# Experts of a small mixture: the second product with the expert's matrix standing still, rows packed and turned in pairs

## The chip, the cores and the metric

The kernel runs on one core of one Trainium2 chip. The metric is the device time of the whole program in microseconds (us), the median of several runs. The core has five engines that work side by side and are held together by semaphores: TensorE (PE in the profile, with PEld for the loading of the stationary operand), VectorE (DVE), ScalarE (ACT), GpSimd (POOL) and SyncE (SP, whose queue carries most DMAs).

## The reference, cut to what matters

The program is one block of a network: a token-pruning attention and, after it, a layer with 8 experts. The change is in the expert layer:

```python
# x: T = 16 * 3136 tokens of D = 64; E = 8 experts, F = 256, C = ceil(1.25 * T / E) = 7840 seats each
idx = argmax(softmax(x @ gate_w + gate_b)); prb = the largest probability
pos = the token's number among those of its expert; kept = pos < C
buf[idx, pos] = x                                         # where kept
hmid = relu(einsum('ecd,edf->ecf', buf, w1) + b1)         # 64 -> 256
ybuf = einsum('ecf,efd->ecd', hmid, w2) + b2              # 256 -> 64
y = nan_to_num(ybuf[idx, pos] * prb * kept, 0, 1e4, -1e4)
out = x + y
```

All of it is fp32.

## The kernel before, in words

The program is six stages, one after the other: `constants`, `rank`, `merge`, `attend`, `project` and `experts`. The stage before the last, `project`, writes every token's row to its seat in a buffer in memory, `xbuf`: 64 numbers to feed the expert (its normalised row), 64 to add the result to, its number, and its probability (130 fp32 in a row).

`experts` (from L1811) goes through the 8 x 7840 seats in 56 chunks of 1120 seats, 7 to an expert. A chunk is one tile `xg` of 112 partitions x 10 seats x 130 numbers, loaded by SP (L1850); there are three such tiles, and a load waits until the chunk three before is finished. The ten seats per partition are worked in three units: two of four seats (two pairs) and one of two (one pair), `XUNITS` = (0, 2), (4, 2), (8, 1). So there are 168 units, numbered m, and unit m = 3c is the first of chunk c.

PE does per unit: `turn` (L1864 to L1874), which turns rows of 112 seats x 64 into columns, by small matmuls against the identity, two per pair, the halves of a pair on the lower and upper 64 partitions of `psX`; `hidden` (L1876 to L1887), the first product, with `w1` standing still and 224 (or 112) columns of seats moving, into `psH`; `outputs` (L1889 to L1900), the second product, in which 112 seats of `hT` stand still and the 64 columns of `w2` move, two accumulated matmuls for each of the unit's four (or two) seats, into `psY`. A matmul of fp32 is two records in the trace. The order is written out by hand, one or two units ahead:

```python
for m in range(-2, UNITS):
    if m + 2 < UNITS: turn(m + 2)
    if 0 <= m + 1 < UNITS: hidden(m + 1)
    if m >= 0: outputs(m)
```

ACT copies `psX` to `xT` (`take`, L1919) and adds the bias b1 and rectifies `psH` into `hT` (`rectify`, two ACTIVATEs a unit, L1928). DVE does per chunk: two additions of the bias b2 out of `psY`, five seats each, into `v` (L1948); the seats' token numbers as integers (`ids`, L1954); `v` times the probability (L1956); the limiting of `nan_to_num` (L1958 to L1962); the sum with the old row into `yo` (L1963), which marks the chunk `finished`. POOL then scatters the chunk's ten columns of seats to the output by token number, ten indirect DMAs (L1970). `yo` and `ids` are double: DVE waits until the scatters of two chunks before have landed (`sent`). Each engine works through its instructions in order.

The stage before has a turn of the kind that the change brings in: at L1622 it turns two seats at a time by one `transpose` of 112 x 128.

Of the kernel before, what the change touches and what calls it, by code (L numbers as in the profile page):

```python
# [21 lines left out]
ALU = mybir.AluOpType  # L22
# [4 lines left out]
TP = 112  # L27
# [169 lines left out]
LAPS = 4  # L197
# [3 lines left out]
def rank(nc, k, d):  # L201
# [3 lines left out]
    with ExitStack() as ctx:  # L205
# [24 lines left out]
        (x_in, centred, squared, varied, rooted, normed, summed, meaned, gated, gtb_made, weighted,  # L230
         maxed, max_turned, max_one, max_all, sum_one, sum_all, probbed, prob_turned, prob_out,
         prob_stored, prob_in, indexed, compared, added, taken, started, blanked, cleared, row_counted) = (sem("r_" + x) for x in (
             "x_in", "centred", "squared", "varied", "rooted", "normed", "summed", "meaned", "gated",
             "gtb_made", "weighted", "maxed", "max_turned", "max_one", "max_all", "sum_one", "sum_all",
             "probbed", "prob_turned", "prob_out", "prob_stored", "prob_in", "indexed",
             "compared", "added", "taken", "started", "blanked", "cleared", "row_counted"))
        scattered, laid = ([sem(f"r_{x}{u}") for u in range(LAPS)] for x in ("scattered", "laid"))
# [1573 lines left out]
def experts(nc, k, d):  # L1811


    with ExitStack() as ctx:
# [8 lines left out]
        b2 = sb("e_b2", [TP, E, C])  # L1823
        xg = [sb(f"e_xg{i}", [TP, XG, XW]) for i in range(3)]
        xT = [sb(f"e_xT{u}", [2 * C, HALF_WIDE]) for u in range(2)]
        hT = [sb(f"e_hT{u}", [128, 2, 2, HALF_WIDE]) for u in range(2)]
        v, lim, lim2 = (sb(x, [TP, XG, C]) for x in ("e_v", "e_lim", "e_lim2"))
# [3 lines left out]
        psX = [ps(f"e_psX{u}", [2 * C, 512]) for u in range(2)]  # L1831
        psH = [ps(f"e_psH{u}", [128, 2, 512]) for u in range(2)]
        psY = [ps(f"e_psY{i}", [TP, 512]) for i in range(2)]
        loaded, turned, x_out, hid, relud, outed, y_taken, finished = (sem("e_" + x) for x in (
            "loaded", "turned", "x_out", "hid", "relud", "outed", "y_taken", "finished"))
        x_in = [sem(f"e_x_in{i}") for i in range(3)]
        sent = [sem(f"e_sent{u}") for u in range(2)]
# [8 lines left out]
        def _(sp):  # L1846
# [16 lines left out]
        def _(pe):  # L1863
            def turn(m):  # L1864
                c, first, pairs = place(m)
                if first == 0:
                    pe.wait_ge(x_in[c % 3], 16 * (c // 3 + 1))
                if m >= 2:
                    pe.wait_ge(x_out, m - 1)
                for r in range(pairs):  # L1870
                    for h in range(2):
                        mm = pe.matmul(psX[m % 2][h * C:(h + 1) * C, r * TP:(r + 1) * TP], xg[c % 3][:, first + 2 * r + h, 0:C],  # L1872
                                       k.ident[0:TP, 0:TP], start=True, stop=True)
                mm.then_inc(turned, 1)  # L1874
# [14 lines left out]
            def outputs(m):  # L1889
                c, first, pairs = place(m)  # L1890
                e = c // XC
# [12 lines left out]
            for m in range(-2, UNITS):  # L1904
# [4 lines left out]
                if m >= 0:  # L1909
                    outputs(m)  # L1910
# [135 lines left out]
```

## Time and profile before

| | us |
|---|---|
| median of 3 runs | 11282.8 (11269.25 to 11288.11) |
| span of the profiled execution, first to last instruction (no other time is given for it) | 11986.8 |
| PE busy in the span | 8145.6 (68%) |
| DVE busy | 8965.6 (75%) |
| ACT busy | 7583.6 (63%) |
| POOL busy | 2313.2 (19%) |
| mean granted clock of TensorE | 0.634 |

The span is the whole program in one profiled execution. "Busy" of PE counts pipelined matmuls, whose ends are modelled, so the distance from the start of one group of matmuls to the start of the next says more than a duration. The granted clock is a share of the full 2.4 GHz: 0.50 is 1.2 GHz. Rows of the order of time give the start in us from the span's start, the time that a merged group of like instructions took, the engine, and in brackets the idle time before it and what ended it.

### The profile page before, as it was taken

Reading aid. Unit: us, or ns where it says so; the run is one execution under the profiler, and the core shown is the slowest. Engines: PE = TensorE matmul, PEld = TensorE weight load, DVE = VectorE, ACT = ScalarE, POOL = GpSimd, SP = SyncE. Lnnn points to the kernel's source line nnn. Section 1 sums busy time; section 2 is a strip of 40 time slices with the busy share of each in tenths; the row PEclk is TensorE's granted clock in tenths of the full one; section 3 lists DMA queues with packets and bytes.
Section 4 is the critical chain, followed back from the end, with each engine's and each line's share of the span. In section 5 each row is a group of like instructions: output and inputs, shape, how many; then the busy total and the mean of one; then the engine's idle time right before and its main releaser. Section 6 shows DMA issues by size and latency. Waiting matters only on the chain. (4 is left out here: it accounts for less than half of the span.)

```text
span 11986.8 us, 168121 instructions
## 1 busy us (share of the span) xinstructions
PE 8145.6 (68%) x45265; PEld 5303.1 (44%) x45265; DVE 8965.6 (75%) x25592; ACT 7583.6 (63%) x12361; POOL 2313.2 (19%) x1944
## 2 busy tenths in 40 slices
PE   6666688838676667678785777766677663445887
PEld 5656455524343334344443444433344332334666
DVE  7777566669898888889898898888889885442232
ACT  5666222249797778789896898977789781221221
POOL 4555122200000000000000000000000002664554
PEclk9999866656556566565665665665656565555555
DMA  3222111100000000000000000000000002331111
GB/s 97 80 80 75 22 25 25 24 18 16 13 18 12 15 12 17 14 15 18 18 15 14 17 15 18 17 12 15 11 18 17 12 15 51 87 73 44 42 42 28
DMA packets 669956, 352.71 MB, mean 29 GB/s; under 512 B 587281, under 2 KB 605680, under 8 KB 665056
## 3 DMA queue, kind: packets, MB, share of 16 engines
q1 hardware_dynamic: 607920, 242.84, 9.2%
q0 software_dynamic: 58624, 60.72, 1.9%
q10 hardware_dynamic: 2384, 37.11, 0.8%
q8 instruction: 441, 7.23, 0.2%
q14 instruction: 587, 4.81, 0.1%
HBM read 200.20 MB, written 147.72 MB: 29 GB/s over the span
## 5 line engine op out<-in xcount | busy, mean ns | idle before, releaser
L1185 PE MATMUL a_psT<-a_qt,a_kt 74*122 74x366 bf16 x3456 | 1573.3, 455 | 1142.8 <-ACT a_pT L1266 733.7
L1274 ACT ACTIVATE a_junk<-a_s,a_aim 122x1097 bf16<-122x1097 f32 x1152 | 1380.6, 1214 | 734.3 <-DVE a_s L1417 734.3
L1266 ACT ACTIVATE a_pT<-a_psT 122x732 f32<-122x732 f32 (+1 forms) x1920 | 1373.9, 716 | 672.8 <-PE a_psT L1188 452.9
L1350 DVE MAX8 a_near<-a_below 122x8 f32<-122x274 f32 (+1 forms) x4608 | 1699.7, 430 | 0.1
L1188 PEld LDWEIGHTS a_psT<-a_weigh,a_drops 122*122 122x122 bf16 x10368 | 1594.1, 193 | 197.1
L1343 DVE SCALAR_TENSOR_TENSOR a_below<-a_s,a_te,a_signs 122x1097 f32<-122x1097 f32 x1152 | 1547.1, 1352 | 131.7 <-remote 130.8
L1188 PE MATMUL a_psT<-a_weigh,a_drops 122*122 122x122 bf16 x10368 | 1541.4, 276 | 0.0
L1185 PEld LDWEIGHTS a_psT<-a_qt,a_kt 74*122 74x122 bf16 x3456 | 622.8, 180 | 1859.7 <-issue 1847.4
L1201 PE MATMUL a_psO<-a_pT,a_v 122*32 122x366 f32 x6912 | 1410.5, 702 | 8.6 <-ACT a_pT L1266 8.6
L1274 ACT ACTIVATE a_signs<-a_s,a_te 122x1097 bf16<-122x1097 f32 x1152 | 1400.8, 1219 | 4.4 <-DVE a_te L1335 4.4
L1274 ACT ACTIVATE a_junk<-a_s,a_te 122x1097 bf16<-122x1097 f32 x1152 | 1391.8, 1212 | 0.0
L1515 POOL DMA_DIRECT2D a_dst<-o x15 | 13.8, 918 | 6751.5 <-DMA o<-a_o 6751.5
L1417 DVE TENSOR_SCALAR_CACHE_REDUCE a_s<-a_psS 122x512 f32<-122x512 f32 (+1 forms) x1280 | 889.9, 726 | 262.1 <-PE a_psS L1168 114.5
L301 ACT ACTIVATE r_spill<-r_greater 112x3136 bf16<-112x3136 bf16 (+26 forms) x432 | 687.0, 1591 | 445.0 <-DVE r_greater L477 349.1
L1157 PE MATMUL a_psS<-a_k,a_q 72*122 72x512 bf16 x640 | 408.8, 639 | 771.8 <-DVE a_s L1417 737.9
L382 POOL DMA_INDIRECT xs<-r_xl,r_idx x448 | 658.9, 1471 | 556.3 <-DVE r_idx L499 424.7
L1291 ACT ACTIVATE a_drops<-a_s,a_raw 122x1097 bf16<-122x1097 f32 x640 | 718.3, 1211 | 3.1 <-DVE a_bad L1389 3.1
L359 PE MATMUL r_pk<-r_minus,r_greater 112*112 112x1 bf16 x6048 | 601.4, 232 | 162.5 <-DVE r_greater L477 139.1
L1417 DVE TENSOR_SCALAR_CACHE_REDUCE a_s<-a_psT 122x512 f32<-122x512 f32 (+1 forms) x1024 | 703.1, 724 | 0.0
L359 PEld LDWEIGHTS r_pk<-r_minus,r_greater 112*112 112x112 bf16 x6048 | 585.2, 211 | 183.2 <-issue 177.0
L1970 POOL DMA_INDIRECT out<-e_yo,e_ids x560 | 545.2, 974 | 562.2 <-DVE e_yo L1963 392.7
L1948 DVE TENSOR_TENSOR e_v<-e_psY,e_b 112x320 f32<-112x320 f32 x112 | 55.1, 492 | 799.3 <-remote 453.0
(375 smaller groups left out, 15344.5 us busy)
## 6 DMA issues: line engine op xcount, KB each, us to landing
xbuf<-r_blank ACTq DMA_DIRECT2D x16, 1990.6 KB
e_xg<-xbuf SPq DMA_DIRECT2D x56, 568.8 KB
r_bc<-pr SPq DMA_DIRECT2D x16, 1372.0 KB, 7.1
a_k<-kT SPq DMA_DIRECT2D x384, 51.5 KB
a_q<-qT SPq DMA_DIRECT2D x384, 51.5 KB
a_kt<-kT SPq DMA_DIRECT2D x384, 51.5 KB
a_qt<-qT SPq DMA_DIRECT2D x384, 51.5 KB
r_xt<-in_x SPq DMA_DIRECT2D x16, 784.0 KB
```

Source lines behind the costliest of these rows:

```text
L301: act.activation(spill[(u + j) % 2][:, j * TP:N], greater[j % MARKS][:, j * TP:N], ACT.Copy, accum_out=cnt[:, 1, j:j + 1]).then_inc(row_co ...
L359: mm = pe.matmul(pk[:, m:m + 1], greater[j % MARKS][:, m * TP:(m + 1) * TP], minus[:, :], start=False, stop=m == NT - 1 and j == NT - 2)
L382: pool.indirect_dma_start(out=d.xs, out_offset=bass.IndirectOffsetOnAxis(ap=idxs[u][:, j:j + 1], axis=0), in_=xls[u][:, j, :], in_offset=N ...
L1185: pe.matmul(out[:, x, 0:CW], kt[q][:, u * QP:(u + 1) * QP], qt[q][:, c * CW:(c + 1) * CW], start=True, stop=False)
L1188: mm = pe.matmul(out[:, x, t * QP:(t + 1) * QP], drops[:, c * CT + t, u * QP:(u + 1) * QP], weigh[:, :], start=False, stop=t == CT - 1)
L1201: mm = pe.matmul(psO[at:at + VC, 0:CW], vh[q][:, u, :], pT[(PER * c + u // 2) % RING][:, u % 2, :], start=g == 0, stop=g == TRIPLES - 1)
L1266: act.activation(pT[j % RING][:, 0:w, :], psT[(q + j) % 2][:, 0:w, 0:CW], ACT.Exp).then_inc(exped, 1)
L1274: act.activation(out[:, :], s_[:, t, :], ACT.Sign, bias=at[:, t:t + 1], scale=-1.0, accum_out=total[:, t:t + 1]).then_inc(counted[r], 1)
L1291: act.activation(drops[:, m, 0:MN], sc[o][:, m, :], ACT.Relu, bias=raw[:, m:m + 1], scale=-1.0).then_inc(act_masked, 1)
L1343: dve.scalar_tensor_tensor(out=below[t % 3][:, :], in0=sc[o][:, t, :], scalar=te[o][:, t:t + 1], in1=signs[t][:, :], op0=ALU.subtract, op1 ...
L1350: mx = dve.max(near[:, t, g, :], below[t % 3][:, EDGES[g]:EDGES[g + 1]])
L1417: dve.tensor_scalar(sc[o][:, t, a:b], banks[i][:, 0:b - a], 1.0, None, ALU.mult, ALU.max, accum_out=peaks[:, i, t:t + 1]).then_inc(evacuat ...
```

## The change

Five things are done, all in `experts`:

- DVE copies the 64 input numbers of each seat of a chunk into a packed tile `xs` (two of them) ahead of the turning (`pack`). PE's turn of a chunk waits for `packed` instead of the load. In DVE's order the pack of chunk c+1 comes at the head of chunk c, before its multiplications.
- A pair is turned by one `transpose` of 112 x 128 instead of two matmuls.
- In the second product the 128 x 64 piece of `w2` stands still and the unit's 224 (or 112) columns of `hT` move, four matmuls a unit; the two halves of a pair go to the lower and upper 64 partitions of `psY`.
- ACT adds the bias b2 while it takes `psY` to `yT` (`bring`), and PE turns `yT` back in pairs by `transpose` into `psV` (`back`), one unit later.
- DVE multiplies by the probability straight out of `psV`, unit by unit. Its two additions of b2 and the multiplication of the whole chunk are gone. b2 is loaded as a column for each expert, twice.

`psX` and `psY` are single now, `psV` is double. The diff also reorders the declaration of semaphores in `rank`, which computes nothing. Cut to its core:

```diff
@@ experts, SP
+                sp.dma_start(b2[h * C:(h + 1) * C, :], d.b2.rearrange("e c -> c e"), allow_slow_non_contiguous=True).then_inc(loaded, 16)
-            sp.dma_start(b2[:, :, :].rearrange("p e n -> p (e n)"),
-                         d.b2.rearrange("(a e) n -> a (e n)", a=1).partition_broadcast(TP)).then_inc(loaded, 16)
@@ experts, PE
                 if first == 0:
-                    pe.wait_ge(x_in[c % 3], 16 * (c // 3 + 1))
-                if m >= 2:
-                    pe.wait_ge(x_out, m - 1)
+                    pe.wait_ge(packed, c + 1)
+                if m >= 1:
+                    pe.wait_ge(x_out, m)
                 for r in range(pairs):
-                    for h in range(2):
-                        mm = pe.matmul(psX[m % 2][h * C:(h + 1) * C, r * TP:(r + 1) * TP], xg[c % 3][:, first + 2 * r + h, 0:C],
-                                       k.ident[0:TP, 0:TP], start=True, stop=True)
+                    mm = pe.transpose(psX[:, r * TP:(r + 1) * TP],
+                                      xs[c % 2][:, first + 2 * r:first + 2 * r + 2, :].rearrange("p j c -> p (j c)"),
+                                      k.ident[0:TP, 0:TP])
                 mm.then_inc(turned, 1)
@@
                 pe.wait_ge(relud, 2 * (m + 1))
-                for g in range(2 * pairs):
-                    half, at = divmod(XG * c + first + g, XU)
-                    r, h = divmod(g, 2)
-                    if at == 0 and half >= 2:
-                        pe.wait_ge(y_taken, half - 1)
-                    for i in range(2):
-                        mm = pe.matmul(psY[half % 2][:, at * C:(at + 1) * C], hT[m % 2][:, i, h, r * TP:(r + 1) * TP],
-                                       w2[:, e, i, :], start=i == 0, stop=i == 1)
+                if m >= 1:
+                    pe.wait_ge(y_out, m)
+                for i in range(2):
+                    for h in range(2):
+                        mm = pe.matmul(psY[h * C:(h + 1) * C, 0:n], w2[:, e, i, :], hT[m % 2][:, i, h, 0:n],
+                                       start=i == 0, stop=i == 1)
                 mm.then_inc(outed, 1)
+            def back(m):
+                c, first, pairs = place(m)
+                pe.wait_ge(y_out, m + 1)
+                if m >= 2:
+                    pe.wait_ge(v_made, m - 1)
+                for r in range(pairs):
+                    mm = pe.transpose(psV[m % 2][:, r * 2 * C:(r + 1) * 2 * C], yT[m % 2][:, r * TP:(r + 1) * TP], k.ident[:, :])
+                mm.then_inc(backed, 1)
+            for m in range(-2, UNITS + 1):
                 if m + 2 < UNITS:
                     turn(m + 2)
                 if 0 <= m + 1 < UNITS:
                     hidden(m + 1)
-                if m >= 0:
+                if 0 <= m < UNITS:
                     outputs(m)
+                if m >= 1:
+                    back(m - 1)
@@ experts, ACT
+            def bring(m):
+                act.wait_ge(outed, m + 1)
+                if m >= 2:
+                    act.wait_ge(backed, m - 1)
+                act.activation(yT[m % 2][:, 0:n], psY[:, 0:n], ACT.Identity, bias=b2[:, e:e + 1]).then_inc(y_out, 1)
+            for m in range(-2, UNITS):
+                if m + 2 < UNITS:
+                    take(m + 2)
+                if 0 <= m + 1 < UNITS:
+                    rectify(m + 1)
+                if m >= 0:
+                    bring(m)
@@ experts, DVE
+            def pack(c):
+                dve.wait_ge(x_in[c % 3], 16 * (c // 3 + 1))
+                if c >= 2:
+                    dve.wait_ge(turned, PER_CHUNK * (c - 1))
+                dve.tensor_copy(xs[c % 2][:, :, :], xg[c % 3][:, :, 0:C]).then_inc(packed, 1)
+            pack(0)
             for c in range(CHUNKS_ALL):
-                for g in range(2):
-                    dve.wait_ge(outed, PER_CHUNK * c + PER_CHUNK - 1 + g)
-                    dve.tensor_tensor(v[:, g * XU:(g + 1) * XU, :], psY[g][:, 0:XU * C].rearrange("p (j c) -> p j c", c=C), bias, ALU.add).then_inc(y_taken, 1)
+                if c + 1 < CHUNKS_ALL:
+                    pack(c + 1)
+                for u, (first, pairs) in enumerate(XUNITS):
+                    m = PER_CHUNK * c + u
+                    dve.wait_ge(backed, m + 1)
+                    tiles = slice(first, first + 2 * pairs)
+                    dve.tensor_tensor(v[:, tiles, :], psV[m % 2][:, 0:2 * pairs * C].rearrange("p (j c) -> p j c", c=C),
+                                      x[:, tiles, 2 * C + 1].unsqueeze(2).to_broadcast([TP, 2 * pairs, C]),
+                                      ALU.mult).then_inc(v_made, 1)
                 if c >= 2:
                     dve.wait_ge(sent[c % 2], 16 * XG * (c // 2))
-                dve.wait_ge(x_in[c % 3], 16 * (c // 3 + 1))
                 link.after(dve.tensor_copy(ids[c % 2][:, :], x[:, :, 2 * C]), 9)
-                dve.wait_ge(y_taken, 2 * c + 2)
-                link.then(dve.tensor_tensor(v[:, :, :], v[:, :, :], x[:, :, 2 * C + 1].unsqueeze(2).to_broadcast([TP, XG, C]),
-                                            ALU.mult))
+                dve.wait_ge(v_made, PER_CHUNK * (c + 1))
                 link.after(dve.tensor_scalar(lim[:, :, :], v[:, :, :], FMAX, 1e4, ALU.is_gt, ALU.mult), 9)
```

## Rows read from the trace of the kernel before

**Rows 1.** Busy time by stretches: us, then PE, PEld, DVE, ACT, POOL, clock, DMA, GB/s.

```profile
10890.00:11987.00 1097.00, 876.23 (x4704) 710.38 (x4704) 316.21 (x560) 222.53 (x504) 545.19 (x560) 0.52 0.14 39
```

**Rows 2.** Groups of instructions by line, stretch of the experts: busy us, mean ns, idle.

```profile
L1899 PE MATMUL e_psY<-e_w,e_hT 128*112 128x64 f32 x2240 | 462.6, 387 | 92.0 <-issue 57.9 <-ACT e_hT L1928 33.0
...
L1948 DVE TENSOR_TENSOR e_v<-e_psY,e_b 112x320 f32<-112x320 f32 x112 | 55.1, 492 | 799.3 <-remote 453.0 <-PE e_psY L1899 241.7 <-issue 104.6
...
L1956 DVE TENSOR_TENSOR e_v<-e_v,e_xg 112x640 f32<-112x640 f32 x56 | 46.3, 826 | 1.2
...
L1919 ACT ACTIVATE e_xT<-e_psX 128x224 f32<-128x224 f32 x112 | 40.1, 358 | 529.7 <-remote 281.4 <-PE e_psX L1872 213.2 <-issue 35.0
...
L1960 DVE TENSOR_SCALAR e_fin<-e_v 112x640 int32<-112x640 f32 x56 | 27.2, 485 | 0.0
```

**Rows 3.** Order of time on PE over one chunk, from one turn to the next.

```profile
11146.69 1.02 PE L1872 MATMUL e_psX<-ident,e_xg 112*64 112x112 f32 x8
11147.63 1.20 PE L1884 MATMUL e_psH<-e_xT,e_w 64*128 64x112 f32 x8
11148.76 3.25 PE L1899 MATMUL e_psY<-e_w,e_hT 128*112 128x64 f32 x16
11151.94 1.01 PE L1872 MATMUL e_psX<-ident,e_xg 112*64 112x112 f32 x8
11152.89 1.86 PE L1884 MATMUL e_psH<-e_xT,e_w 64*128 64x224 f32 x8
11154.68 1.75 PE L1899 MATMUL e_psY<-e_w,e_hT 128*112 128x64 f32 x8
...
11161.91 1.26 PE L1872 MATMUL e_psX<-ident,e_xg 112*64 112x112 f32 x8
```

**Rows 4.** Order of time on POOL, one scatter near the end.

```profile
11965.28 0.94 POOL L1970 DMA_INDIRECT out<-e_yo,e_ids  x1 [0.30 <-issue]
```

**Rows 5.** Order of time on DVE: the last result of the stage.

```profile
11958.36 0.82 DVE L1963 TENSOR_TENSOR e_yo<-e_lim,e_xg 112x640 f32<-112x640 f32 x1
```

**Rows 6.** Busy time by stretches: a dense stretch and the slow one behind it.

```profile
11274.00:11314.00 40.00, 39.55 (x220) 32.35 (x216) 16.39 (x29) 9.47 (x21) 17.96 (x19) 0.50 0.16 45
11314.00:11331.00 17.00, 8.31 (x35) 6.53 (x36) 0.00 (x0) 1.51 (x3) 11.18 (x12) 0.50 0.16 51
```

**Rows 7.** Order of time on PE in the stage before: packed transposes.

```profile
10428.23 3.02 PE L1622 MATMUL p_psT<-ident,p_y 112*128 112x112 f32 x14
```

**Rows 8.** Order of time on DVE: the limiting and the sum of one chunk.

```profile
11124.92 0.49 DVE L1958 TENSOR_SCALAR e_lim<-e_v 112x640 f32<-112x640 f32 x1
...
11127.90 0.82 DVE L1963 TENSOR_TENSOR e_yo<-e_lim,e_xg 112x640 f32<-112x640 f32 x1
```

**Rows 9.** Order of time on PE early in the stage, one chunk apart.

```profile
10910.88 1.00 PE L1899 MATMUL e_psY<-e_w,e_hT 128*112 128x64 f32 x8
...
10918.24 1.03 PE L1884 MATMUL e_psH<-e_xT,e_w 64*128 64x224 f32 x8
...
10919.20 1.00 PE L1899 MATMUL e_psY<-e_w,e_hT 128*112 128x64 f32 x8
```

**Rows 10.** Stretches with the granted clock (third number from the end), and PE before rises.

```profile
10764.80:10768.20 3.40, 3.34 (x13) 2.78 (x14) 2.36 (x11) 0.54 (x1) 2.49 (x4) 0.50 0.15 44
10768.20:10771.60 3.40, 0.92 (x6) 0.50 (x6) 2.66 (x10) 0.54 (x1) 2.49 (x4) 1.00 0.16 44
...
10766.49 2.75 PE L1622 MATMUL p_psT<-ident,p_t 112*128 112x112 f32 x14
...
10898.96 1.76 PE L1872 MATMUL e_psX<-ident,e_xg 112*64 112x112 f32 x16 [66.51 <-DMA e_xg<-xbuf]
...
10904.70:10908.10 3.40, 3.40 (x38) 2.98 (x37) 0.00 (x0) 1.82 (x4) 0.00 (x0) 1.00 0.00 0
...
10932.00:10935.40 3.40, 1.90 (x7) 1.11 (x7) 0.00 (x0) 0.00 (x0) 2.49 (x4) 0.50 0.06 17
10956.00:10985.00 29.00, 28.25 (x158) 23.19 (x159) 11.25 (x20) 6.91 (x15) 16.18 (x17) 0.50 0.12 33
```

More of the change, by code:

```diff
@@ L1822, in experts @@
         b1 = sb("e_b1", [128, E, F // 128])
-        b2 = sb("e_b2", [TP, E, C])
+        b2 = sb("e_b2", [2 * C, E])
         xg = [sb(f"e_xg{i}", [TP, XG, XW]) for i in range(3)]
@@ L1826, in experts @@
         hT = [sb(f"e_hT{u}", [128, 2, 2, HALF_WIDE]) for u in range(2)]
+        yT = [sb(f"e_yT{u}", [2 * C, HALF_WIDE]) for u in range(2)]
         v, lim, lim2 = (sb(x, [TP, XG, C]) for x in ("e_v", "e_lim", "e_lim2"))
@@ L1830, in experts @@
         yo = [sb(f"e_yo{u}", [TP, XG, C]) for u in range(2)]
-        psX = [ps(f"e_psX{u}", [2 * C, 512]) for u in range(2)]
+        xs = [sb(f"e_xs{u}", [TP, XG, C]) for u in range(2)]
+        psX, psY = (ps(x, [2 * C, 512]) for x in ("e_psX", "e_psY"))
         psH = [ps(f"e_psH{u}", [128, 2, 512]) for u in range(2)]
-        psY = [ps(f"e_psY{i}", [TP, 512]) for i in range(2)]
-        loaded, turned, x_out, hid, relud, outed, y_taken, finished = (sem("e_" + x) for x in (
-            "loaded", "turned", "x_out", "hid", "relud", "outed", "y_taken", "finished"))
+        psV = [ps(f"e_psV{u}", [TP, 512]) for u in range(2)]
+        sent = [sem(f"e_sent{u}") for u in range(2)]
+        loaded, packed, turned, x_out, hid, relud, outed, y_out, backed, v_made, finished = (sem("e_" + x) for x in (
+            "loaded", "packed", "turned", "x_out", "hid", "relud", "outed", "y_out", "backed", "v_made", "finished"))
         x_in = [sem(f"e_x_in{i}") for i in range(3)]
-        sent = [sem(f"e_sent{u}") for u in range(2)]
         block = ctx.enter_context(nc.Block())
@@ L1890, in outputs @@
                 c, first, pairs = place(m)
[L1891 removed]
+                e, n = c // XC, pairs * TP
                 pe.wait_ge(relud, 2 * (m + 1))
[L1893 to L1904 removed]
+                if m >= 1:
[4 more added lines that the diff above has]
+                                       start=i == 0, stop=i == 1)
+                mm.then_inc(outed, 1)
+            def back(m):
[6 more added lines that the diff above has]
+                mm.then_inc(backed, 1)
+            pe.wait_ge(loaded, 16 * 6)
+            for m in range(-2, UNITS + 1):
                 if m + 2 < UNITS:
@@ L1918, in take @@
                     act.wait_ge(hid, m - 1)
-                act.activation(xT[m % 2][:, 0:pairs * TP], psX[m % 2][:, 0:pairs * TP], ACT.Copy).then_inc(x_out, 1)
+                act.activation(xT[m % 2][:, 0:pairs * TP], psX[:, 0:pairs * TP], ACT.Copy).then_inc(x_out, 1)
             def rectify(m):
@@ L1929, in rectify @@
                                    bias=b1[:, e, i:i + 1]).then_inc(relud, 1)
-            act.wait_ge(loaded, 16 * 5)
-            take(0)
-            for m in range(UNITS):
-                if m + 1 < UNITS:
-                    take(m + 1)
-                rectify(m)
+            def bring(m):
+                c, first, pairs = place(m)
+                e, n = c // XC, pairs * TP
+                act.wait_ge(outed, m + 1)
+                if m >= 2:
+                    act.wait_ge(backed, m - 1)
+                act.activation(yT[m % 2][:, 0:n], psY[:, 0:n], ACT.Identity, bias=b2[:, e:e + 1]).then_inc(y_out, 1)
+            act.wait_ge(loaded, 16 * 6)
+            for m in range(-2, UNITS):
[5 more added lines that the diff above has]
+                    bring(m)
         @block.vector
```

25 lines of the change are left out of this document (9 added, 16 removed).

## The prediction

> **What bounds the kernel now.** The profile's busy times by stretches come first [rows 1]: the change lies in the last stage, the experts, which fills the last 1097 us of the span of 11986.8, and there PE is busy 876 us, POOL 545, DVE 316, ACT 223. PE is the bound. The groups of the stage [rows 2] say with what: the second product (L1899, 2240 records with 64 columns moving past a 112-wide stationary piece) has 462.6 us of it, more than half. The order of time [rows 3] shows one whole chunk with no idle time on PE: from the turn at 11146.69 to the next chunk's at 11161.91 are 15.22 us. In it a turn of two pairs takes 0.95 (start to start of the next part); the first product 1.79 or, for one pair, 1.13; the second product 3.18 for two pairs and about 1.7 for one. POOL needs 0.94 us and 0.30 of idle time for each of the ten scatters of a chunk [rows 4], 12.4 in all, so it is the next bound. DVE is far from it, but its work has an order, and that will matter.
>
> Two things spoil this plain picture. First, 56 chunks of 15.22 us are 852 us, and the stage took 1060 from the first turn (10898.96 [rows 10]) to the end of the last result (11959.2 [rows 5]), 18.9 a chunk: between dense stretches of 40 us (220 records) stand stretches of some 15 to 17 us in which PE gets 35 records done, at idle times that nothing releases, while POOL scatters at its usual pace [rows 6]. This is 3.7 us a chunk. Second, the span is 704 us above the median of the runs, 11282.8. The profiled execution loses 6% that the runs don't, and the slow stretches follow each dense burst of PE records (they come in the stage before too). I take them for a loss of the profiled execution, so that in the runs a chunk costs about 15.2 us, and work out the sum for both readings.
>
> **The change, part by part.** All prices are at TensorE's lower clock first, since the granted clock is 0.50 (1.2 GHz) over nearly all of the stage.
>
> Turns. Ten small matmuls a chunk (20 records, 0.95 us for eight) become five transposes of 112x128. The stage before does just this: 14 of them in 3.02 us, one record each, 0.205 us from start to start [rows 7]. So 0.41, 0.41 and 0.2: 1.0 us instead of 2.5.
>
> First product. Untouched: 1.79 + 1.79 + 1.13 = 4.7 us.
>
> Second product. Per unit four matmuls of fp32 (8 records), the 64-wide stationary matrix in either half of the array's columns, 224 or 112 columns moving. That is the shape of the old turn of two pairs (64 wide, 112 moving, 8 records, two halves of the output's partitions): 0.94 us [rows 3]. For 224 columns I add what 112 more columns cost the first product, 1.79 - 1.13 = 0.66: 1.6 us. So 1.6 + 1.6 + 0.94 = 4.1 us instead of 8.05. Lower bound 3.9 (no more per column than at the first product's start), upper bound 8: if the halves do not run beside each other, each record costs twice.
>
> Turning back. Five transposes of 128x112, by the same row 1.0 us, new.
>
> PE's own work is then 1.0 + 4.7 + 4.1 + 1.0 = 10.9 us a chunk.
>
> ACT gets a third evacuation per unit, 0.36 us for 224 columns (0.45 with a bias) by the old one [rows 2]: a chunk's ACT work goes from 4.1 to 5.3 us. In PE's order it lies between the second product of unit m and that of unit m+1, behind a back turn, a turn and a first product (2.6 us at the lower clock), against 1.2 for the rest of the rectification and 0.45 for itself. Cost nothing; if the clock were full throughout, those 2.6 us would be 1.4, and it might cost some 0.3 us a unit. With psX and psY single, PE waits for these evacuations too, with the same cover.
>
> DVE. Per chunk it gains a pack (112x640, fp32; nearest rows the one-source operations on 112x640, 0.49; upper bound the two-source one, 0.83) and three multiplications out of PSUM (about 0.42, 0.42 and 0.29 by the line through 0.49 for 320 and 0.83 for 640 elements), and loses two additions of 0.49 and a multiplication of 0.83 [rows 2]. Near zero in sum. **Its order is the cost.** The pack of chunk c+1 stands behind all of chunk c-1's work on DVE. That ends with limits and additions that take 3.80 us from the first (L1958) to the end of the last (L1963) [rows 8], and begins only when PE has turned back the last unit of chunk c-1. In PE's order this back turn is the last thing of iteration m = 3c, and the very next thing, the turn of unit 3c+3, waits for `packed` >= c+2. So once a chunk PE stands still: last transpose's end about 0.15 after the point where it would go on, multiplication 0.29, the ids and wait 0.15, 3.80, pack 0.5, and semaphores 0.15 in all: 5.05 us. Bounds 4.7 and 5.6 (a pack at 0.83, a later ids). Before, the turn waited for the load alone, and all of DVE's tail lay beside PE. Queued behind the waiting turn are the first and second products and, through them, ACT; all stand still. POOL is not held: its 12.4 us go on.
>
> So a chunk costs 10.9 + 5.05 = 16.0 us at the lower clock, against 15.2: slower by 0.8.
>
> **The clock.** At the higher clock (1.00, that is 2.4 GHz) early in the stage the first product takes 0.96 us and a chunk 8.32 [rows 9]. So PE's parts shrink to 0.54 or 0.55. Will it be granted? From 10956 to 10985 PE is busy 28.25 of 29 us with the old mix of parts, and the clock stays at 0.50 [rows 10]. Two rises show another history: the one at 10904.7 came after turns and first products alone, with no second product between; the one at 10768.2, in the stage before, after products of 224 columns and then packed transposes [rows 10]. The old second product, 112 columns loaded for 64 moved, stands before neither. After the change PE's bursts are made of first products, second products with 224 columns moving, and transposes: all of the kinds that preceded the rises. The Trainium skill says under "TensorE: Matmul & The Clock Gate", Part 1, that sustained matmul activity brings the full clock. The 29 us above contradict it for the old mix; by that rule alone the kernel before would already be at POOL's pace and the change would bring nothing.
>
> From the two rises I expect one in each burst. It comes late: PE had worked 5.7 us in the one case (10898.96 to 10904.7) and 3.4 in the other (10764.8 to 10768.2); I take the middle, 4.5. It is lost again in each standstill: when a slow stretch began at 10930, the clock was at 0.50 from 10932 on [rows 10]. A chunk is then 4.5 + (10.9 - 4.5) x 0.54 = 8.0 us of work, and with 5.05 of standstill 13.0; POOL's 12.4 fit in just.
>
> Edges: b2 is loaded twice, element by element, in place of one broadcast; the stage waits for the slowest load of all. The pipeline is one step deeper. I add 2 us, between -3 and +8.
>
> **The sum.** (13.0 - 15.2) x 56 = -123, +2: -121 us, so 11282.8 - 121 = **11162 us**. Against the profiled execution itself the base is 18.9 us a chunk. The new PE work has 116 records a chunk instead of 168, which in 13.0 us is the mean rate of the old stage (168 in 18.9), so few slow stretches should be left: its span falls by about 300 us (5.3 a chunk), to some 11690.
>
> **The rivals.**
>
> *The clock stays low.* For: the stage before has transposes in plenty at 0.50 and its clock hardly rises. Against: there they stand beside products of 8 and 64 columns. Price: 16.0 - 15.2 = 0.8 x 56 + 2 = +47, 11330 us. It decides at the pack's wait: as soon as the rise comes later than about 9.4 us into a burst (9.4 + 1.5 x 0.54 + 5.05 = 15.2) the chunk is slower than before. In the same direction speaks the Trainium skill, "TensorE: Matmul & The Clock Gate", Part 4 (PE-mode transpose): transposes do not count toward the full clock. The rise at 10768.2 came 1.7 us into a row of transposes, which speaks against it. Chance 0.18.
>
> *The slow stretches are in the runs too.* Then the base is 18.9 and the change gives, with 0.6 for stretches that are left, (13.6 - 18.9) x 56 = -297, 10986 us. For: nothing in the stretches looks like a recorder's doing. Against: the 704 us between span and median have to be somewhere. Chance 0.11.
>
> *The column halves run one after the other.* The second product stays near 8 us, work 14.7, with the rise 4.5 + 5.5 + 5.05 = 15.05: no change, some 11277 us. Against: the old turn's rows. If the clock also stays low, 19.75 a chunk and +255. Chance 0.07.
>
> *POOL takes over.* If the clock is kept over the standstill, work is 5.9 us, the chunk 11 and POOL's 12.4 rule: (12.4 - 15.2) x 56 + 2 = -155, 11128 us. Against: the fall at 10932. Chance 0.08.
>
> **How the numbers follow.** The forecast has the remaining 0.56; its own range, with rises between 3.3 and 7 us and a standstill of 4.7 to 5.6, is 11128 to 11255. For 8 in 10 the range has to take in the low clock and part of the stretches' case: 11050 to 11335. A measurement of this kernel can tell 0.2% from no change, about 23 us. Faster by more: 0.56 + 0.11 + 0.08, less a little for late rises: 0.73. Slower: the low clock and a part of the halves: 0.19. Same: 0.08.
>
> **What would show it.** In the profile after: transposes as single records, 0.2 us apart at 0.50; the second product's 8 records in about 1.6 us at 0.50 and 0.9 at 1.00; PE idle about 5 us before the turn of each chunk's first unit, released by the pack on DVE; the granted clock of the stage between 0.6 and 0.8; POOL busy near 90% of the loop. A clock of 0.50, or a standstill much longer than 5.6 us, proves the forecast wrong; so does a second product above 3 us.

## The result, and the profile after

The changed kernel takes 11230.84 us (median of 9 runs, 11210.15 to 11243.92), the kernel before in the same series 11282.8 (9 runs, 11227.06 to 11313.02). The two medians are 52 us apart. The ratio of the two kernels over these runs is **0.9948, 95% interval 0.9933 to 0.9964**: 0.52% or 59 us faster, where 121 us were forecast. The absolute time lies in the stated range of 11128 to 11255 us, at its slow end. The profiled execution has a span of 11242.2 us; that of before had 11986.8.

Busy time by stretches of the changed kernel: 650 us of the loop over the chunks, and three pieces of 6.8 us in it (columns as in [rows 1]):

```profile
10500.00:11150.00 650.00, 426.06 (x2774) 272.98 (x2770) 255.79 (x524) 239.18 (x575) 504.84 (x477) 0.75 0.20 56
10810.40:10817.20 6.80, 5.25 (x26) 3.54 (x28) 1.89 (x4) 1.95 (x5) 5.28 (x6) 0.50 0.36 96
10817.20:10824.00 6.80, 3.66 (x34) 2.18 (x30) 3.46 (x8) 3.05 (x7) 5.28 (x6) 1.00 0.02 0
10824.00:10830.80 6.80, 5.20 (x26) 3.49 (x28) 1.94 (x4) 1.95 (x5) 5.28 (x6) 0.50 0.29 86
```

PE was busy 28.25 of 29 us before [rows 10]; now it is busy 426 of 650 us. The clock goes up and down once a chunk, 0.75 in the mean. This execution has no slow stretches.

Order of time of the changed kernel over one chunk, from the turn that ends one standstill to the turn that ends the next:

```profile
10811.95 0.63 PE L1872 MATMUL e_psX<-ident,e_xs 112*128 112x112 f32 x2 [4.75 <-DVE e_xs L1966]
10812.52 1.20 PE L1885 MATMUL e_psH<-e_xT,e_w 64*128 64x112 f32 x8
10813.65 1.76 PE L1898 MATMUL e_psY<-e_hT,e_w 128*64 128x224 f32 x8
10815.34 0.68 PE L1908 MATMUL e_psV<-ident,e_yT 128*112 128x128 f32 x2
10815.81 0.58 PE L1872 MATMUL e_psX<-ident,e_xs 112*128 112x112 f32 x2
10816.32 1.43 PE L1885 MATMUL e_psH<-e_xT,e_w 64*128 64x224 f32 x8
...
10819.63 0.98 PE L1898 MATMUL e_psY<-e_hT,e_w 128*64 128x224 f32 x8
...
10820.54 0.32 PE L1908 MATMUL e_psV<-ident,e_yT 128*112 128x128 f32 x1
...
10820.90 0.29 DVE L1977 TENSOR_TENSOR e_v<-e_psV,e_xg 112x128 f32<-112x128 f32 x1 [1.79 <-PE e_psV L1908]
10821.11 0.16 DVE L1982 CAST e_ids<-e_xg 112x10 uint32<-112x10 f32 x1
10821.30 0.55 DVE L1984 TENSOR_SCALAR e_lim<-e_v 112x640 f32<-112x640 f32 x1
10821.32 1.04 POOL L1996 DMA_INDIRECT out<-e_yo,e_ids  x1 [0.31 <-issue]
...
10822.67 1.53 POOL L1996 DMA_INDIRECT out<-e_yo,e_ids  x1 [0.30 <-issue]
...
10824.32 0.82 DVE L1989 TENSOR_TENSOR e_yo<-e_lim,e_xg 112x640 f32<-112x640 f32 x1
10824.51 1.45 POOL L1996 DMA_INDIRECT out<-e_yo,e_ids  x1 [0.30 <-issue]
10825.06 0.49 DVE L1966 COPY e_xs<-e_xg 112x640 f32<-112x640 f32 x1
10825.60 0.64 PE L1872 MATMUL e_psX<-ident,e_xs 112*128 112x112 f32 x2 [4.74 <-DVE e_xs L1966]
```

The chunk takes 13.65 us (10811.95 to 10825.60): a burst of 8.9 us on PE, then the standstill of 4.75 that the prediction worked out from DVE's order, with DVE's tail from 10821.30 to the pack lying in it. A second product of two pairs takes 1.69 us at the start of a burst (10813.65 to 10815.34) and 0.91 at its end; before it took 3.18 [rows 3]. The clock rises 5.25 us into the burst, at 10817.2, and so it does, within 0.05 us, in all 47 bursts between 10500 and 11150. From the first result on DVE to the last the mean distance is 13.50 us: the 54 before the last are 13.3 to 13.7, and the last is only 5.8, since PE has no further pack to wait for. The waits show the same standstill, 53 times, in the stretch from 10480 to 11200:

```profile
DVE e_v L1977 <- PE e_psV L1908: 430.4, 158, 4.2
...
PE e_psX L1872 <- DVE e_xs L1966: 250.7, 53, 4.8
```

### The profile page after: what moved, and what is told of

It reads as the page before. It is cut to its first block and busy times, and to the rows that moved or that the text cites. A ratio compares the mean times of both kernels' runs of the same rounds, so it can differ in the third digit from the quotient of the medians.

```text
span 11242.2 us, 165877 instructions
## 1 busy us (share of the span) xinstructions
PE 7747.9 (69%) x43809; PEld 4910.0 (44%) x43809; DVE 8949.4 (80%) x25648; ACT 7642.9 (68%) x12529; POOL 2366.2 (21%) x1944
## 5 line engine op out<-in xcount | busy, mean ns | idle before, releaser
L1996 POOL DMA_INDIRECT out<-e_yo,e_ids x560 | 592.1, 1057 | 214.6 <-issue 170.5
L1157 PEld LDWEIGHTS a_psS<-a_k,a_q 72*122 72x122 bf16 x640 | 115.5, 181 | 1065.6 <-issue 1063.1
```

The costliest lines, as they stand in the source:

```text
L1996: pool.indirect_dma_start(out=d.out, out_offset=bass.IndirectOffsetOnAxis(ap=ids[c % 2][:, q:q + 1], axis=0), in_=yo[c % 2][:, q, :], in_o ...
```

## The experiments

"Chunk" is the usual distance of two chunks in the loop, "mean" that of the first result on DVE to the last, over 55. The clock is that from 10500 to 11150 us, for the kernels without limiting and with the pack early and half of the scatters that from 10500 to 11100 and to 10900. Each trace is of one execution.

| kernel | time, us | ratio to before | chunk (mean), us | clock in the loop |
|---|---|---|---|---|
| before again | 11295.52 | 1.0014 [0.9997, 1.0031] | 13.5 or 15.2 (14.13) | 0.53 |
| pack early | 11223.89 | 0.9941 [0.9922, 0.9961] | 13.4 (13.27) | 0.75 |
| old turns, new second product | 11221.09 | 0.9949 [0.9930, 0.9969] | 13.4 (13.26) | 0.77 |
| new turns, old second product | 11298.92 | 1.0006 [0.9987, 1.0024] | 14.6 (14.54) | 0.50 |
| pack early, no limiting | 11168.95 | 0.9900 [0.9878, 0.9922] | 13.0 (12.78) | 0.76 |
| after, half of the scatters | 11218.3, one run | | 13.65 (13.50) | 0.75 |
| before, half of the scatters | 11231.2, one run | | 15.2, at the end 8.3 (13.80) | 0.50, then 1.00 |
| pack early, half of the scatters | 10936.87, one run | | 8.4 to 9.1 (8.72) | 0.90 |
| limiting by unit in PSUM | 11186.66 | 0.9929 [0.9904, 0.9955] | 13.08 (12.81) | 0.78 |
| limiting by unit in SBUF | 11204.83 | 0.9942 [0.9921, 0.9964] | 13.32 (13.02) | 0.78 |
| in PSUM, sum in parts | 11185.49 | 0.9904 [0.9884, 0.9924] | 13.0 (12.80) | 0.77 |
| in PSUM again | 11198.12 | 0.9911 [0.9892, 0.9931] | 13.07 (12.83) | 0.79 |

The kernels ran in four groups, each on one chip with the kernel before beside it: the first four rows (kernel before 11290.75 us), the next four (11270.86), then two (11278.44) and two (11300.24).

**The kernel before, again.** What does a chunk cost before, and are the slow stretches [rows 6] real?

> The kernel before once more, for a second profile of it. The profiled execution on record had a span of 11986.8 us with slow stretches of PE, 704 above the runs; the changed kernel's had none (11242.2). Theory A (a recording loss, and in the runs PE also gets the higher clock at times): span about 11280, no slow stretches, a chunk of 14.6 to 14.8 us on average (58 us over 56 chunks above the changed kernel's 13.65), granted clock of the last stage clearly above 0.52. Theory B (PE stays at the lower clock in the runs too): a chunk of 15.2, the stage 852 us, so that something else in the program must have become slower by about 30 us with the change. Theory C: the slow stretches come again and the runs agree with them.

The profiled execution took 11256.62 us at a span of 11254.9, with no slow stretch. So the 704 us were lost in that one profiled execution, and not in runs. This is theory A in kind, with a mean chunk below its 14.6 to 14.8. Stretches of time, PE around the second rise of the clock, and a wait:

```profile
10474.00:10630.00 156.00, 155.85 (x864) 129.43 (x865) 62.45 (x108) 42.01 (x93) 118.38 (x115) 0.50 0.17 47
10670.00:11140.00 470.00, 470.00 (x2596) 389.74 (x2597) 184.88 (x317) 125.82 (x277) 322.36 (x320) 0.50 0.19 54
11147.00:11176.00 29.00, 28.38 (x285) 23.84 (x283) 17.48 (x31) 14.38 (x32) 21.44 (x21) 1.00 0.23 69
...
10631.67 1.02 PE L1872 MATMUL e_psX<-ident,e_xg 112*64 112x112 f32 x8
10632.61 1.86 PE L1884 MATMUL e_psH<-e_xT,e_w 64*128 64x224 f32 x8
10634.41 1.00 PE L1899 MATMUL e_psY<-e_w,e_hT 128*112 128x64 f32 x8
...
10666.40 1.02 PE L1872 MATMUL e_psX<-ident,e_xg 112*64 112x112 f32 x8 [1.94 <-DMA e_xg<-xbuf]
...
DVE e_ids L1954 <- DMA out<-e_yo,e_ids: 59.1, 13, 7.8
```

At 0.50 a chunk takes 15.2 us, with PE the bound. But in three phases (10436 to 10474, 10634 to 10665, 11146 to 11177) the clock is at 1.00. PE then does a chunk in 8.3 us and gets ahead, until DVE waits for POOL's scatters (last line, of the waits) and PE for a load that those hold back. Each of the three phases ended during such a standstill of PE, of 1.6 to 2.0 us. The results come 13.5 us apart, POOL's own pace, until its backlog is gone. Over 55 chunks the mean is 14.13, not 15.2. The runs scatter accordingly: of 69 of the kernel before, the seven with a mean clock of 0.635 or 0.636 over the whole program took 11320 us in the mean, the nine with 0.642 to 0.644 11247.

The rises in the middle of the loop have one place in the order of work. At 10634.4 and 11146.4 here, at 11136.8 in the first profile of before, and at 11122.2 in the kernel before with half of the scatters (below), PE had just done a turn of two pairs and a first product of 224 columns: 2.7 us, the longest stretch of a chunk without a second product. Why one chunk brings a rise and the next dozens don't, no run shows.

**The pack ahead of the limiting.** It takes the cause away that the prediction gave for the standstill: DVE packs chunk c+2 before it limits chunk c.

```diff
+            pack(1)
             for c in range(CHUNKS_ALL):
-                if c + 1 < CHUNKS_ALL:
-                    pack(c + 1)
                 for u, (first, pairs) in enumerate(XUNITS):
...
+                if c + 2 < CHUNKS_ALL:
+                    pack(c + 2)
                 if c >= 2:
                     dve.wait_ge(sent[c % 2], 16 * XG * (c // 2))
```

> The changed kernel with the pack of chunk c+2 put ahead of DVE's limiting of chunk c, so that PE's turn no longer waits for the limiting. Theory A (the standstill of 4.75 us sets the chunk, POOL needs 12.45): the chunk falls from 13.65 to about 12.5, the kernel to about 11165, ratio to before 0.990. Theory B (POOL's own work is 13.6 us a chunk, since scatters beside DVE's limiting take up to 1.5 us instead of 0.94; it is already busy without a gap): the standstill goes, but PE then waits elsewhere, for POOL through DVE; chunk 13.3 to 13.7, ratio 0.994 to 0.996 as with the change.

Theory B held: 11223.89 us, a gain of 0.07% on the change, within the intervals. Waits, 10480 to 11150:

```profile
DVE e_ids L1983 <- DMA out<-e_yo,e_ids: 236.9, 50, 5.2
...
PE e_psX L1872 <- DVE e_xs L1966: 194.2, 51, 4.3
```

Now DVE waits for the scatters in every chunk, and POOL has no gap beyond the 0.30 us between scatters. PE's wait for the pack is still there, because the pack now waits for the load (147.1 us in 50 waits) and the load for a result that POOL holds back. POOL's chunk is 13.4 us, not the 12.4 of the prediction, and the trace shows why:

```profile
10905.45 0.94 POOL L1997 DMA_INDIRECT out<-e_yo,e_ids  x1 [0.30 <-issue]
...
10907.63 0.82 DVE L1988 TENSOR_TENSOR e_lim<-e_lim 112x640 f32<-112x640 f32 x1
10908.14 1.12 POOL L1997 DMA_INDIRECT out<-e_yo,e_ids  x1 [0.30 <-issue]
...
10909.40 0.83 DVE L1990 TENSOR_TENSOR e_yo<-e_lim,e_xg 112x640 f32<-112x640 f32 x1
10909.56 1.47 POOL L1997 DMA_INDIRECT out<-e_yo,e_ids  x1 [0.30 <-issue]
```

A scatter of 0.94 us takes 1.1 to 1.5 beside DVE's limiting and sum.

**The two halves of the change by themselves.** Old turns with the new second product (the turn and its wait as before the change, no pack), and new turns with the old second product.

```diff
-                    pe.wait_ge(packed, c + 1)
+                    pe.wait_ge(x_in[c % 3], 16 * (c // 3 + 1))
...
-                    mm = pe.transpose(psX[:, r * TP:(r + 1) * TP],
...
+                    for h in range(2):
+                        mm = pe.matmul(psX[h * C:(h + 1) * C, r * TP:(r + 1) * TP], xg[c % 3][:, first + 2 * r + h, 0:C],
```

> The changed kernel with the turns of before (two matmuls a pair, straight from the loaded tile, no pack). This also removes the standstill. PE's work at the lower clock is 10.9 + 1.5 = 12.4 us a chunk, about 6.8 at the higher. Theory A (POOL 12.45): chunk 12.5, about 11165 us. Theory B (POOL 13.6 with DVE beside it): 13.2 to 13.7, about 11220, no worse than with the change, so packing and turning in pairs brings nothing by itself. The granted clock tells whether the new second product alone brings the higher clock: above 0.6 if so.

> The kernel before with only the pack and the turning in pairs; the second product as before. PE's work at the lower clock is 15.2 - 1.5 = 13.7 us a chunk; the pack behind DVE's limiting leaves a wait of about 1 us before the first turn of a chunk (6.0 us of DVE after the last second product, 4.6 us of other work on PE). Theory A (the clock stays low without the new second product): chunk 14.5 to 14.8, about as before or 20 us faster, clock near 0.5. Theory B (transposes bring the higher clock): chunk near POOL's bound, 12.5 to 13.7, 60 us faster or more.

Busy time of the loop, first of the old turns with the new second product, then of the new turns alone:

```profile
10500.00:11150.00 650.00, 468.03 (x3565) 293.21 (x3565) 235.02 (x490) 243.81 (x586) 502.13 (x486) 0.77 0.20 56
```

```profile
10500.00:11150.00 650.00, 620.92 (x3072) 516.16 (x3072) 268.49 (x487) 181.23 (x400) 448.42 (x446) 0.50 0.18 53
```

The second product in its new form brings the higher clock and the whole gain; packing and turning in pairs brings nothing (1.0006). How much of the gain is the clock's in the kernel with the old turns isn't shown: its PE work at 0.50, 12.4 us by the estimate in its expectation, would fit into POOL's 13.4 too. With the new turns alone a chunk at 0.50 takes 14.6 us instead of 15.2, but the phases at 1.00 are gone: its stage has not one rise.

**Without the limiting.** The pack early, and the five operations of `nan_to_num` left out of the computation. DVE also waits for its own sum before the next chunk's multiplications.

```diff
-                link.after(dve.tensor_scalar(lim[:, :, :], v[:, :, :], FMAX, 1e4, ALU.is_gt, ALU.mult), 9)
...
-                dve.tensor_tensor(y[:, :, :], lim[:, :, :], x[:, :, C:2 * C], ALU.add).then_inc(finished, 1)
+                dve.tensor_tensor(y[:, :, :], v[:, :, :], x[:, :, C:2 * C], ALU.add).then_inc(finished, 1)
```

> The kernel with the early pack, and the limiting (nan_to_num: five operations on DVE for each chunk) left out of the computation, so that DVE does only the sum there. Theory A (POOL's 13.4 us a chunk are ten scatters at 1.245 plus about 0.9 us by which scatters are stretched beside DVE's limiting): the chunk falls to 12.5 to 12.7 us, the kernel by some 45 us against the early pack, to about 11180; the scatters take 0.94 nearly all. Theory B (the stretch comes from the loads or the scatters' own traffic): the chunk stays at 13.3 to 13.4.

The chunk falls from 13.4 to 13.0 us, not to 12.5 or 12.7: one scatter in nearly each chunk still takes 1.49 us, beside the sum. The stage gets shorter by 0.49 x 55 = 27 us. The medians are 55 us apart, but they are of two chips; by the ratios to the kernel before it is 0.41%, 46 us. What exceeds the 27 isn't explained. In the profiled execution the first result came 44 us earlier than with the pack early, and such starts lay anywhere from 10430 to 10475 in the profiled kernels.

**Half of the scatters.** POOL's loop and the two waits count to 5 instead of 10, so half of the output is not written. It takes POOL out of the question.

```diff
-                for q in range(XG):
+                for q in range(XU):
...
-                    dve.wait_ge(sent[c % 2], 16 * XG * (c // 2))
+                    dve.wait_ge(sent[c % 2], 16 * XU * (c // 2))
```

> The changed kernel with five of the ten scatters of each chunk left out (half of the output is not written). POOL then needs about 7 us a chunk. Theory A (the wait of PE for the pack behind DVE's limiting, 4.75 us, and the clock that rises and falls in each chunk set the 13.65): no change, 13.65 us a chunk, about 11240. Theory B (POOL sets it, being busy without a gap): the chunk falls below 13, to 12.5 or less.

> The kernel before with half of the scatters left out. Theory A (the clock of before falls because POOL holds PE back at 13.5 us a chunk against PE's 8.3, and then doesn't come back for long, as the old second product does not bring it): with POOL at 7 us nothing holds PE at the start, the higher clock that is granted at 10436 in the profile of before stays, and a chunk takes 8.3 us: the kernel falls to about 10920. Theory B (the higher clock ends by itself with this mix): 15.2 us a chunk for most of the stage, about 11300.

> The kernel with the early pack and half of the scatters left out: what the new PE work can do when neither POOL nor the pack holds it. Theory A (the new work brings and keeps the higher clock): 10.9 x 0.54 = 5.9 us of PE a chunk, but DVE's 6.9 and the load that follows each finished chunk hold it: 7 to 8.5 us a chunk, about 10880. Theory B (its transposes do not keep the clock): 10 to 11 us a chunk, about 11060.

In the changed kernel nothing moves: 13.65 us a chunk with POOL half idle (theory A). Standstill and clock set its pace. In the kernel before the two stretches are these:

```profile
10500.00:11120.00 620.00, 620.00 (x3426) 514.69 (x3424) 229.93 (x410) 165.97 (x366) 192.40 (x205) 0.50 0.16 45
11122.00:11210.00 88.00, 88.00 (x887) 74.10 (x885) 59.93 (x108) 43.44 (x95) 52.33 (x50) 1.00 0.23 63
```

620 us of PE without a gap, at 0.50, and then, with the same instructions, 88 us at 1.00 and 8.3 us a chunk. So for most of the stage it is theory B. In this one execution the clock rose once and stayed up for the 92 us to the end of PE's work; in the second profile of the kernel before, with all ten scatters, each phase ended after 31 to 38 us, at a standstill. The third kernel, with the pack early, runs at 8.4 to 9.1 us a chunk, and its clock is at 1.00 for most of the time:

```profile
10500.00:10900.00 400.00, 335.89 (x2644) 216.13 (x2646) 242.06 (x501) 227.06 (x546) 238.65 (x227) 0.90 0.27 77
```

The mean of 8.7 us lies a little above the 7 to 8.5 of theory A, and PE is busy for 84% of it. So half of POOL's scatters are worth 4.7 us of each of the 13.4.

**What lengthens a scatter.** Old turns and new second product, with the limiting done unit by unit: once on the rows as they lie in PSUM after the multiplication by the probability, once on a copy of them in SBUF (`src` is then `v[:, tiles, :]`).

```diff
-                    dve.tensor_tensor(v[:, tiles, :], psV[m % 2][:, 0:2 * pairs * C].rearrange("p (j c) -> p j c", c=C),
+                    p = psV[m % 2][:, 0:2 * pairs * C].rearrange("p (j c) -> p j c", c=C)
+                    src, low, high, ok = p, lim[:, tiles, :], lim2[:, tiles, :], fin[:, tiles, :]
+                    link.then(dve.tensor_tensor(src, p, x[:, tiles, 2 * C + 1].unsqueeze(2).to_broadcast([TP, 2 * pairs, C]),
...
+                    link.after(dve.tensor_scalar(low, src, FMAX, 1e4, ALU.is_gt, ALU.mult), 9)
...
+                    dve.copy_predicated(low, ok, src).then_inc(v_made, 1)
```

> The changed kernel with the turns of before and without the pack (as e2), and with the limiting done unit by unit, on the gated rows left in PSUM: of each unit's six operations of DVE the multiplication, the two comparisons, the finite test and the predicated copy read PSUM, only the addition of the two limits and, once a chunk, the last sum read SBUF on both sides. Theory A (a scatter of POOL is stretched from 0.94 to about 1.5 us beside operations of DVE that read SBUF, and hardly beside those that read PSUM, as it isn't beside the multiplications of the changed kernel): POOL's ten scatters and their gaps fall from 13.35 us a chunk in e2 to 12.7 to 13.0, and the time by 56 x 0.35 to 0.65, 20 to 36 us, to 11185 to 11201. Theory B (any operation of DVE, or the write of the result, stretches it): POOL's chunk stays at 13.3 to 13.6 and the time within 10 us of e2's 11221.

> The control for e8: the same order of work, the limiting unit by unit, but on a copy of the gated rows in SBUF, as in the kernels before. Theory A (operands in SBUF stretch the scatters): POOL's chunk 13.3 to 13.6 us and the time within 12 us of e2's 11221, so 20 to 36 us above e8. Theory B (what counts is only how the operations are spread over the chunk): POOL's chunk equals that of e8, whatever it is, and the two times agree within 10 us.

Order of time on DVE and POOL, of the kernel with the limiting in PSUM and then of the one in SBUF:

```profile
10900.85 0.82 DVE L1985 TENSOR_TENSOR e_yo<-e_lim,e_xg 112x640 f32<-112x640 f32 x1
10900.95 1.54 POOL L1992 DMA_INDIRECT out<-e_yo,e_ids  x1 [0.30 <-issue]
...
10902.58 0.41 DVE L1976 TENSOR_SCALAR e_lim<-e_psV 112x256 f32<-112x256 f32 x1
10902.79 0.94 POOL L1992 DMA_INDIRECT out<-e_yo,e_ids  x1 [0.30 <-issue]
```

```profile
10909.03 0.28 DVE L1977 TENSOR_SCALAR e_fin<-e_v 112x256 int32<-112x256 f32 x1
10909.10 1.02 POOL L1992 DMA_INDIRECT out<-e_yo,e_ids  x1 [0.30 <-issue]
...
10911.53 0.44 DVE L1979 COPY_PREDICATED e_lim<-e_fin,e_v 112x256 f32<-112x256 int32 x1
10911.67 1.10 POOL L1992 DMA_INDIRECT out<-e_yo,e_ids  x1 [0.30 <-issue]
```

In PSUM nine scatters of ten take 0.94, in SBUF seven. The comparison itself is slower from PSUM (0.41 us against 0.29 in the mean), but nothing waits for it. The chunk is 13.08 against 13.32, the time 18 us less on the same chip: theory A, a little below its size. The runs of the two overlap (11169 to 11209 and 11192 to 11212), so the chunk says it more surely than the time.

The scatter beside the sum remains. So the sum was cut into three parts, beside the same kernel once more:

```diff
-                dve.tensor_tensor(y[:, :, :], lim[:, :, :], x[:, :, C:2 * C], ALU.add).then_inc(finished, 1)
+                for u, (first, pairs) in enumerate(XUNITS):
+                    tiles = slice(first, first + 2 * pairs)
...
+                    ins = dve.tensor_tensor(y[:, tiles, :], lim[:, tiles, :], x[:, tiles, C:2 * C], ALU.add)
```

> As e8, with the last sum of a chunk, the only operation beside which a scatter of POOL still took 1.54 us instead of 0.94 (0.82 us on 112x640, both sources in SBUF), cut into three of 112x256, 112x128 and 112x256. The additions of the limits in e8, of the same kind on 112x256 (0.41 us), had no longer scatter beside them. Theory A (a scatter waits only for a long operation of two SBUF sources, and the short ones fit between its accesses): POOL's chunk falls from 13.0 to between 12.4 and 12.6, and the time by 56 x 0.45 to 0.6, 25 to 34 us, against e8 on the same chip. Theory B (the scatter waits as long as any such operations run beside it, however cut): POOL's chunk stays at 13.0 to 13.2, and the time within 8 us of e8's.

> e8 again, unchanged, on the chip of e10 so that the two can be compared: POOL's chunk 13.0 us as before by both theories; the time a ratio of about 0.993 to the kernel before.

```profile
10899.70 1.16 DVE L1989 TENSOR_TENSOR e_yo<-e_lim,e_xg 112x256 f32<-112x256 f32 x3
10899.76 1.18 POOL L2000 DMA_INDIRECT out<-e_yo,e_ids  x1 [0.30 <-issue]
...
10902.42 0.42 DVE L1978 TENSOR_TENSOR e_lim<-e_lim 112x256 f32<-112x256 f32 x1
10902.49 1.16 POOL L2000 DMA_INDIRECT out<-e_yo,e_ids  x1 [0.30 <-issue]
```

Theory B: no scatter takes 1.5 us any more, but three in each chunk take 1.05 to 1.18, and the chunk stays at 13.0 us. The 13 us between the two times are more than the theory's 8, but lie within what the runs scatter. Of the kernels that do the whole computation those with the limiting in PSUM are the fastest here, 0.9929 and 0.9911 in two series of the one, 0.9904 with the sum in parts, against 0.9948 for the change. The interval of the first overlaps the change's, those of the other two do not; their chunk is 0.6 us shorter than the change's.

## Where the prediction was right, and why it forecast twice the gain

*The second product.* 1.6 us at the lower clock and 0.9 at the higher were forecast, 1.69 and 0.91 came, so the halves don't cost double and that rival is out.

*The standstill.* Right in place and cause. 5.05 us were forecast, 4.75 came.

*The clock.* Right in kind: it rises in each burst and is lost after it. The rise was taken as 4.5 us into the burst, from two rises 3.4 and 5.7 us in [rows 10]; it came at 5.25 (with the pack early, anywhere from 3.5 to 6.6 us in, 5.1 in the mean of 48 bursts). With that the burst would be 5.25 + (10.9 - 5.25) x 0.54 = 8.3 us. It was 8.9. The other 0.6 are parts that were priced too low: two transposes take 0.47 to 0.57 us from start to start at 0.50 instead of 0.41, the second product 1.69, and from 10816.32 to the end of the burst it takes 4.5 us where these prices give 4.2. A burst of 8.9 in place of 8.0 and a standstill of 4.75 in place of 5.05 make the usual chunk 13.65 in place of 13.0; in the mean, which the short last distance lowers, it is 13.50. So the term **"8.0 us of work, and with 5.05 of standstill 13.0"** was 0.5 too low, 28 us over 56 chunks.

The Trainium skill says under "TensorE: Matmul & The Clock Gate", Part 4, that transposes do not count as busy for the clock. The new turns without the new second product agree with it (0.50 throughout), and the old turns without transposes in them got 0.77; but all kernels whose clock rises in each chunk turn back by transposes, so no run tests them alone. Part 1 of that page, that sustained matmul activity brings the full clock, is contradicted again by 470 us and 620 us of unbroken PE work at 0.50.

*The base.* This is the step that failed most: **"in the runs a chunk costs about 15.2 us"**. It holds only at the lower clock. In the second profiled execution it was 14.13 in the mean; that execution was 34 us faster than the median of its series (11256.62 against 11290.75), and if this lies in the stage the median's chunk is some 14.13 + 34 / 56 = 14.7. The prediction's own first rows had shown the clock up early in the stage [rows 9], and the same profile has one more rise, at 11136.8, which the prediction left out:

```profile
11120.00:11136.80 16.80, 16.80 (x92) 13.69 (x92) 5.62 (x10) 4.15 (x11) 5.64 (x6) 0.50 0.13 36
11136.80:11143.70 6.90, 2.53 (x23) 1.88 (x22) 0.00 (x0) 1.42 (x3) 3.77 (x4) 0.99 0.02 0
```

It came out of the old mix, so phases at the higher clock belong to the old kernel too; that the old second product stands before no rise holds only for the two that the prediction named. With a base between 14.1 and 14.7, an estimate from one trace, the 15.2 were too high by 0.5 to 1.1 us a chunk, 28 to 60 us. What is missing is 62 us by the ratio or 69 by the medians. With 28 us for the chunk after and the 2 us of edges that didn't come, 36 to 43 are left for the base, the larger part; that would be a base of 14.4 to 14.6. No run gives it directly, since the clock phases of the kernel before differ from run to run.

*POOL.* Ten scatters at 0.94 and 0.30 were counted, 12.4 us. With DVE's limiting beside them they need 13.4. It did not set the 13.65, as the half number of scatters shows, though in the changed kernel too it has no gap beyond the 0.30 us (ten scatters of 1.061 us in the mean and 0.305 between them are 13.66). It leaves only 0.25 us to be had from the standstill, which the early pack confirmed, and it holds the kernel before to 13.5 us after its rises instead of 8.3. The rival "POOL takes over" and its 11128 us rest on the 12.4 and were 1.0 us a chunk too low. "POOL busy near 90%" was named as a sign; it is busy 78%, since the 0.30 us between scatters don't count.

*ACT* cost nothing, as forecast: between 10480 and 11200 the only wait listed for PE is that for the pack. *Edges:* from the first turn to the first result are 16.4 us in both kernels (10432.6 to 10449.0 before, 10453.4 to 10469.8 after), so the 2 us were not needed. *The slow stretches* are out as a rival; the forecast of a profiled span of 11690 rested on their coming back in part, and they didn't. *The clock stays low* is out for the whole change, and is what happens to the turns alone, though that kernel comes to no change, not to +47 us.

## What to carry to other kernels

A stage that runs at two clocks has no single price: take the base from a second execution, by phase, before taking a difference of it. Where the change puts a wait on one engine, look at the next bound with its neighbours' work beside it: a scatter priced while DVE rests was 8% too cheap, and that bound left almost nothing to gain by removing the wait. To turn a matmul round so that the wide side moves can be worth as much by the clock it brings as by the columns it saves. In the changed kernel the columns save about 3.7 us a chunk at the lower clock (8.05 to 2 x 1.69 + 0.94), less about 1.0 for turning back. The clock saves some 3.1: the 3.7 us that a burst takes after the rise would be 6.8 at the ratio of 0.54. Both are estimates.

## What the runs showed of the hardware that was not expected

- A scatter of POOL (0.94 us) is held by an operation of DVE that it begins within, if that operation reads SBUF with both its sources. The extra time is what was left of the operation, less 0.12 or 0.13 us: 0.61 for 0.73 left beside the sum in the kernel with the limiting in PSUM (mean of 45), 0.48 for 0.60 beside the addition of the limits in the changed kernel (55), 0.16 for 0.29 beside that addition in the kernel with the sum in parts (102). A one-source operation from SBUF to SBUF does it too, 0.08 for 0.21 in the kernel with the limiting in SBUF (48), but by no such simple rule: beside the first comparison of the changed kernel it was 0.11 for 0.52 left in 40 cases and 0.42 for 0.44 in 14. Beside operations that read PSUM it is nothing: 0.00 for 0.40 left beside the multiplication (46), 0.00 for 0.28 beside the finite test (48), both with the limiting in PSUM. The Trainium skill has the mechanism under "SBUF — State Buffer", "SBUF: two separate sides": DVE and GpSimd share a pair of ports that one instruction holds to its end, and descriptors of DMAs issued from GpSimd wait for it. The rows of operations with two sources in SBUF agree, up to the 0.12 us; the prediction had not used it.
- The same instructions of the kernel before run for hundreds of microseconds at 1.2 GHz and then for 30 to 90 at 2.4 GHz (470 and 31 in the second profile, 620 and 92 with half of the scatters), differently in each execution. With the wide second product the clock is regular, and the runs lie closer: 11210 to 11244 us in 9 runs, against 11227 to 11313 before.
- One profiled execution lost 704 us (6%) in slow stretches that no other execution of that kernel showed, though its program was the same.
